# Attention in rounds of two units with shared banks and the division on POOL; alignment path coded by flags on DVE, PE and ACT

## The reference

```python
# layer 1: attention; latents = normalised x, keys and values from context and latents together
q = ln @ Wq                                   # 16 heads of 64
k, v = split(concat([xn, ln]) @ Wkv)          # 256 keys for each of the 64 sequences
w = softmax(q @ k.T / 8)
x = x + (w @ v) @ Wo
# layer 3: dynamic time warping of each context sequence against each x sequence
D = pairwise_euclidean(context, layernorm(x)) # 128 x 128
R[i, j] = D[i, j] + min(R[i-1, j], R[i, j-1], R[i-1, j-1])
# walk back from the last cell: diagonal before up before left on ties,
# and add context row i to output row j for every cell (i, j) on the way
```

## Time and profile before

| | |
|---|---|
| runs (3) | 3696.86, 3699.18, 3698.50 us; median 3698.5 us |
| profiled execution | 3698.72 us, span 3697.0 us |
| PE busy | 3236.4 us, 88% of the span |
| DVE busy | 2700.5 us, 73% |
| ACT busy | 1969.6 us, 53% |
| POOL busy | 1141.7 us, 31% |
| attention | to about 1970 us of the span |
| experts and distances | to about 2964 us |
| alignment | to about 3212 us |

### The profile page before, as it was taken

One profiled execution on the slowest core, in us unless ns is written; L12 is line 12 of the kernel. 1 busy time (PEld: TensorE's weight loads), 2 busy tenths in 40 slices (PEclk: granted clock), 3 DMA queues, 4 the chain that ended last, 5 costly groups with the idle time before them and its releaser, 6 DMA issues. The chain is left out here.

```text
span 3697.0 us, 64710 instructions
## 1 busy us (share of the span) xinstructions
PE 3236.4 (88%) x23172; PEld 2706.9 (73%) x23172; DVE 2700.5 (73%) x5786; ACT 1969.6 (53%) x5061; POOL 1141.7 (31%) x1116
## 2 busy tenths in 40 slices
PE   6999999999999999999996999999999800167786
PEld 5888888888888888888885888888888800055564
DVE  6777777777777777777765655665664979879997
ACT  4565656666565656565653333333333601099996
POOL 2222222222222222222211333333333200058888
PEclk9999999999999999999997999999999955588888
DMA  4000000000000000000002011101101740001101
GB/s 145 4 7 4 7 4 7 7 4 7 4 7 4 7 4 7 4 7 4 7 1 75 30 42 47 47 25 47 47 28 43 223 85 0 6 29 41 35 29 35
DMA packets 104171, 108.01 MB, mean 29 GB/s; under 512 B 7856, under 2 KB 85168, under 8 KB 103856
## 3 DMA queue, kind: packets, MB, share of 16 engines
q1 hardware_dynamic: 103856, 103.88, 9.5%
HBM read 90.75 MB, written 13.11 MB: 28 GB/s over the span
## 5 line engine op out<-in xcount | busy, mean ns | idle before, releaser
L619 POOL TENSOR_TENSOR attention_prob<-attention_prob,attention_inv_sums 128x512 f32<-128x512 f32 x256 | 266.7, 1042 | 1250.8 <-DVE attention_inv_sums L536 1250.8
L423 ACT ACTIVATE attention_prob<-attention_scores,attention_neg_max 128x256 f32<-128x256 f32 x1024 | 471.8, 473 | 142.9 <-DVE attention_neg_max L529 77.5
L406 ACT ACTIVATE attention_k_hi<-attention_proj 128x512 fp32r<-128x512 f32 x256 | 152.9, 597 | 554.5 <-PE attention_proj L277 554.5
L1068 POOL TENSOR_TENSOR experts_hidden_lo<-experts_weighed,experts_hidden_hi 128x512 fp32r<-128x512 f32 x192 | 252.2, 1313 | 551.1 <-ACT experts_hidden_hi L891 551.1
L539 DVE TENSOR_SCALAR attention_prob<-attention_prob,attention_inv_sums 128x256 f32<-128x256 f32 x512 | 398.1, 817 | 9.0
L546 DVE COPY attention_probT<-attention_turned 128x512 f32<-128x512 f32 x256 | 177.1, 692 | 294.9 <-PE attention_heads_out L331 294.9
L891 ACT ACTIVATE experts_hidden_hi<-experts_weighed 128x512 fp32r<-128x512 f32 x192 | 121.4, 632 | 424.1 <-DVE experts_weighed L1020 424.1
L529 DVE TENSOR_REDUCE attention_neg_max<-attention_scores 128x2 f32<-128x512 f32 x512 | 325.1, 675 | 3.4 <-PE attention_scores L303 3.4
L331 PE MATMUL attention_heads_out<-attention_probT,attention_v 128*64 128x128 f32 x4096 | 281.9, 280 | 1.6 <-DVE attention_attT_lo L553 1.6
L1015 DVE TENSOR_TENSOR experts_silu<-experts_silu,experts_spread 128x512 f32<-128x512 f32 x128 | 89.3, 698 | 259.4 <-ACT experts_silu L885 258.3
L315 PE MATMUL attention_turned<-ident,attention_prob 128*128 128x128 f32 x2048 | 265.4, 272 | 4.4 <-DVE attention_prob L539 4.4
(11 more groups left out here) (259 smaller groups left out, 9842.0 us busy)
## 6 DMA issues: line engine op xcount, KB each, us to landing
experts_spread<-shares SPq DMA_DIRECT2D x256, 128.0 KB, 3.0
x_all<-in_x SPq DMA_DIRECT2D x8, 1024.0 KB, 10.7
attention_ctx<-in_ctx SPq DMA_DIRECT2D x32, 256.0 KB, 2.7
distance_ctx<-in_ctx SPq DMA_DIRECT2D x16, 512.0 KB, 4.3
distance_ctxT<-in_ctxT SPq DMA_DIRECT2D x32, 256.0 KB, 4.8
weights_ctx<-in_ctx SPq DMA_DIRECT2D x16, 512.0 KB, 3.9
out<-conv_x_out SPq DMA_DIRECT2D x15, 512.0 KB, 3.0
dist<-distance_dist SPq DMA_DIRECT2D x16, 256.0 KB, 2.5
```

The costliest lines, as they stand in the source:

```text
L423: made = act.activation(prob[:, h, :], scores[e][:, m * 256:(m + 1) * 256], ACT.Exp, bias=neg_max[:, n % 2, 2 * e + m:2 * e + m + 1], accu ...
L619: pool.tensor_tensor(prob[:, 2:4, :], prob[:, 2:4, :], inv[:, n % 2, 2:4].unsqueeze(2).broadcast_to([P, 2, 2 * TOK]), ALU.mult).then_inc(d ...
L1068: pool.tensor_tensor(hid_lo[n % 3][:, :], weighed[n % 2], hid_hi[n % 3][:, :].bitcast(F32), ALU.subtract).then_inc(hid_split, 1)
```

## The change

Attention now goes in 128 rounds of two units. In round `u`, with `n = 2u`, PE does score(n), score(n+1), weigh_values(u-1) for both units of the last round in one group of 32 matmuls, project_k(n+2), project_q(u+1), project_k(n+3), then project_v and turn_probs twice, and in the first round of a pair both outputs of the last pair; turn_inputs stands at the end of the first two rounds of a pair.

The three `proj`, two `scores` and two `turned` banks become one rotation of seven banks `turns`; a user waits for the one seven places earlier. `prob` and `probT` have two buffers each. All four heads are divided on POOL, in one instruction of 1024 columns; DVE only inverts the sums. All four copies of a round from `turned` to `probT` are DVE's; ACT has none. The high and low parts of the weighed heads are made once a round with 512 columns. k has two buffers instead of three, v three homes instead of two buffers. All of norm_a, norm_b and norm_c of the next pair fall in the first round of a pair. x is waited for in four sets.

In the alignment a chunk is coded with flags in bf16: DVE makes `falls` (1152 columns) and `left` (1024) after the chunk; PE exchanges the halves of the partitions with four matmuls into `diag_ps`; six rows into the next chunk DVE makes `moved` (1024) and a multiply-and-add scan `back` (1024); PE takes the differences of neighbours in `back` with four matmuls, and ACT copies them to `rise`. The last chunk is finished after the last row. The ternary work on ACT stands between chunks.

```diff
-            for n in range(LAST + 4):
...
+            for u in range(ROUNDS + 1):
+                n = 2 * u
+                more = u + 1 < ROUNDS
+                if u < ROUNDS:
+                    score(n)
+                    score(n + 1)
+                if u:
+                    weigh_values(u - 1)
+                if more:
+                    project_k(n + 2)
+                    project_q(u + 1)
+                    project_k(n + 3)
+                for j in range(2):
+                    if more:
+                        project_v(n + 2 + j)
+                    if u < ROUNDS:
+                        turn_probs(n + j)
+                for b in outputs_in(u):
+                    output(b)
+                if late_input(u) is not None:
+                    turn_inputs(late_input(u))
...
-            def divide(n):
+            def invert(n):
                 dve.wait_ge(exped, n + 1)
+                if n >= 2:
+                    dve.wait_ge(divided, n - 1)
                 dve.reciprocal(inv[:, n % 2, :], sums[:, n % 2, :]).then_inc(inverted, 1)
-                dve.wait_ge(inverted, n + 1)
-                for h in range(2):
-                    made = dve.tensor_scalar(prob[:, h, :], prob[:, h, :], inv[:, n % 2, h:h + 1], None, ALU.mult)
-                made.then_inc(divided, 1)
...
+                if u < ROUNDS:
                     row_max(n)
+                    row_max(n + 1)
...
+                    if norm_next:
+                        norm_a(p + 1)
+                    invert(n)
+                    invert(n + 1)
+                if more:
                     low_k(n + 2)
+                if u:
+                    low_heads(u - 1)
+                if norm_next:
+                    norm_b(p + 1)
+                if more:
+                    low_q(u + 1)
+                    low_k(n + 3)
+                if u < ROUNDS:
+                    copy_probs(n)
+                    if norm_next:
+                        norm_c(p + 1)
+                    copy_probs(n + 1)
+                for b in outputs_in(u):
+                    add_out(b)
...
+            for u in range(ROUNDS):
+                p, i = divmod(u, QUADS)
+                if p + 1 < PAIRS and not i:
                     inverse_std(p + 1, 0, 4)
+                for n in (2 * u, 2 * u + 1):
+                    pool.wait_ge(inverted, n + 1)
+                    pool.tensor_tensor(prob[n % 2][:, :, :], prob[n % 2][:, :, :],
+                                       inv[:, n % 2, :].unsqueeze(2).broadcast_to([P, QH, 2 * TOK]), ALU.mult
+                                       ).then_inc(divided, 1)
+                if p + 1 < PAIRS and not i:
                     inverse_std(p + 1, 1, 2)
+                if late_input(u) is not None:
+                    low_inputs(late_input(u))
...
                 if (i + 1) % (2 * CH) == 0:
                     dve.wait_ge(row_made, i + 1)
-                    for part in coding:
-                        part(k // CH)
-                if i == N // 2:
+                    compare(k // CH)
+                if i % (2 * CH) == 5 and i > 2 * CH:
+                    trace(k // CH - 1)
+                if i == 84:
                     weights.means(dve)
+            trace(CHUNKS - 1)
```

More of the change, by code:

```diff
@@ L76, in attention @@
     PER_PAIR = 2 * QUADS
+    ROUNDS = LAST // 2
     XC = 8
+    X_SETS = (range(0, 1), range(1, 2), range(2, 4), range(4, 8))
     STAGES, PER_STAGE = 4, INNER // DIM
@@ L295, in score @@
                 pe.wait_ge(k_split, 2 * u + 2)
-                if n:
-                    pe.wait_ge(exped, n)
+                banks = [take_bank("s", 2 * n + e) for e in range(2)]
                 for h in range(QH):
```

430 lines of the change are left out of this document (226 added, 204 removed).

## The result

The changed kernel takes 3593.5 us (median of 4 runs, 3592.0 to 3595.0) against 3698.1 us (4 runs, 3696.9 to 3699.2): ratio 0.972, 95% interval 0.970 to 0.973. The forecast was 3641 with a range of 3570 to 3695: the right sign, inside the range, 47.5 us too long.

What follows compares the result with a forecast made beforehand. PE's own pace was taken to bound attention, DVE's dependent chain the alignment. From 3698.7 us: attention -94, PE standing in first rounds +62, alignment -26, sum -58, hence 3641 us; range 3570 to 3695.

Steps and rivals of the forecast that it cites:

- So about 0.1 goes wherever PE goes into or out of a group of another shape: PE in attention: each entry to or exit from a matmul group of another shape loses about 0.1 us.
- 12.03 + 0.60 = 12.63: Plain attention round on PE: bare work plus shape-change losses in us, 0.76 less than before, bounds 0.6 and 0.85.
- Values 2.05: Bare PE time in us taken for the values products of one two-unit attention round.
- PE stands 2.0 us: Pair's first round, last turning: PE waits for DVE's low q behind normalisations blocked by POOL's divisions; +62 us in total.
- not blocked: Rival: DVE's normalisation passes beside POOL's division, so PE never stands; 3579 us, chance 0.27.
- The two divisions of DVE ... cost nothing and give nothing: Attention round: taking DVE's two divisions off it changes no time, since PE is the bound.
- The values want the last copy at 1.6 and have it at 1.3: Attention round: DVE's last turned copy lands 0.3 us before PE's values need it, the round's smallest slack.
- Start and end of the stage at 0, outputs at +3: Attention: stage ends change nothing (bounds -4 and +4); outputs now following the turning cost 0.1 us a pair, +3.
- Alignment -26: Alignment: DVE's cheaper chunk coding saves 28.7 us, the uncovered last chunk adds 2.2; bounds -17 and -36.
- the 0.3 for the exchange: Alignment's last chunk: the part of PE's exchange, in us, that DVE's `left` does not hide.
- Waits, not shapes: Rival: PE's losses come from semaphore waits before groups, so grouping saves only 13 us; 3722 us, slower, chance 0.11.
- stopped elsewhere: Rival: attention is held up elsewhere, likeliest by late copies before the values; 3679 us, or 3710 with longer division, chance 0.12.

Runs made afterwards that it cites:

- kernels 5: Changed kernel with the next unit's k projection put back between the two units' scores; 3669.9 us, ratio 0.993 to the kernel before.
- 10: Changed kernel with low q and low k ahead of the normalisation, plus values split in two groups with a k projection between them; 3599.0 us, ratio 0.973.
- Kernels 4: Changed kernel with one more, already met, semaphore wait in the middle of each k and v projection; 3592.4 us, ratio 0.972.
- kernel 8: Changed kernel with low q and low k ahead of the normalisation, plus both v projections ahead of both turnings; 3554.3 us, ratio 0.962.
- Kernel 3: Changed kernel with DVE making low q and low k before the normalisation instead of after it; 3550.7 us, ratio 0.961.
- kernel 7: Changed kernel with the division shared again, DVE dividing heads 0 and 1 of each unit, POOL heads 2 and 3; 3563.2 us, ratio 0.964.
- kernel 9: Changed kernel with both low q and low k ahead of the normalisation and the division shared by DVE and POOL; 3547.7 us, ratio 0.959.
- kernel 2: The change's attention with the alignment of the kernel before; 3620.8 us, ratio 0.980.

## Why the prediction was right in sign and 47 us too long

Its mechanisms held, two of its sizes did not.

- **"So about 0.1 goes wherever PE goes into or out of a group of another shape": held in kind, and it is 0.19 for a change.** It was given as 0.1 an entry and 0.1 an exit, with turnings counted as a shape of their own. Six such losses, 0.60, were left in the changed round; three changes at 0.19 are 0.58, so this term came out right in sum. Counted by tile size alone, a round of before has 8 changes (each unit: into the scores, out of them, into the values, out of them) and one of the changed kernel 3 (turning to scores, scores to values, values to k). 5 fewer at (13.39 - 12.42) / 5 = 0.194 each; kernels 5 and 10 give 0.19 by adding two. In the starts it shows as the prediction's 0.1 in and 0.1 out: a score's first interval is 0.22 where the next are 0.12, the one from the last score product to the values is 0.22, and the first of the k behind the values is 0.35 in place of 0.23. Kernels 4 and 10 exclude the waits, kernel 8 the kind of product.
- **"12.03 + 0.60 = 12.63": the failed term.** The bare work is too high. "Values 2.05" is twice the distance from 16 values to the next group, which has a loss at its exit each time; the 0.1 at values to k was then added on top. One group of 32 takes 1.89, and with the k behind it 3.40 in place of 3.54. q was put at 12 x 0.118 = 1.42; its products start 0.113 apart and it takes 1.36. The scores with their losses take 1.64 in place of 1.72, the second k 1.37 in place of 1.39, and the two v and turnings 4.65 in place of 4.56. Together that is the error of 0.21; over 128 rounds 27 us. The 0.97 saved lies outside the bounds that were given for it, 0.6 and 0.85.
- **"PE stands 2.0 us": right in place, releaser and cause, too long by 0.6**, 18 us over 31. POOL's division is 1.90 as taken. But the divisions ran from 6.7 to 10.5 us of the round (which begins at 1019.43), not from 7.05 to 11.15: the sums came earlier, and DVE's instruction between the two divisions did not shove the second by 0.3 (POOL's second lasts 1.94, its first 1.90). Low q landed at 12.9 where the laid out round had 13.8. Kernel 3 shows cause and price (43 us). So the rival *not blocked*, which gave 3579, was wrong in its cause, though at 14.5 us from the measured time it was closer than the forecast. That was luck: it left out a stand of 44 us and saved 27 too little in the plain rounds, and the two errors cancel in part. With nothing standing the time is that of kernel 3, 3551.
- **POOL's division and what stands beside it.** The trace shows DVE's normalisation at 0.86 and 1.98 us beside POOL's divisions, each to 0.15 behind a division's end, and at 0.40 behind them; the rule of the Trainium skill that the second to come waits out the other's instruction ("SBUF — State Buffer", Who interferes with whom) agrees. The trace has 1.90 us for a division of 1024 columns; the 2.6 cycles an element of the Trainium skill ("GPSIMD Engine Reference", 3.1) made it an estimated 2.2, which is too much here. That page's advice, to leave two-input work on DVE, kernel 7 bears out by 30 us for half of the division, through DVE's wait; with low q early (kernel 9) it is worth nothing that shows.
- **"The two divisions of DVE ... cost nothing and give nothing"**: right (kernels 7 and 9). The consequence was not drawn: with that order of DVE, moving them to POOL was all price.
- **"The values want the last copy at 1.6 and have it at 1.3"**: right, with more room. In the round of 1064.68 DVE's last copy ends at 1065.71, 1.0 into it. The page of the changed kernel has 1.0 us of idle for the values in all 128 rounds (L345, released by the copies).
- **Start and end of the stage at 0, outputs at +3:** the sum of the new terms, 128 x 0.97 = 124 less 31 x 1.41 = 44, is 80, and the attention became 80.4 shorter. Nothing is left for either. The stages behind it took 2.1 us more here and about 1.5 less in kernel 2 with the same attention, so no effect of the change on them is shown.
- **Alignment -26: -28.0.** Around the first seven chunks, from row scan to row scan, the coding is 6.11 where it was 9.82. That is 3.71 less, 29.7 for eight (28.7 predicted). The last chunk gave back 1.75 where 2.2 was taken: the wait behind the scan is near the 1.85 predicted, but the 0.3 for the exchange did not come, since its matmuls ran two at a time (below) and were done at 3038.42, with DVE's `left` at 3038.44.
- *Waits, not shapes* (3722) and *stopped elsewhere* (3679 to 3710) did not happen. The one rotation of seven banks and the second buffers of `prob` and `probT` were not run by themselves; the five changes fewer leave no part of the plain round's 0.97 for them.

## What to carry to other kernels

When PE is the bound, count the places where the tile size of its products changes and group by it. In this kernel the count times one measured change gives the round, while kinds of product on the same tile size and waits that are already met cost nothing that showed. A group's measured length holds its entry or exit loss: take that out before adding losses of your own. Before giving work to POOL, look at which of DVE's instructions it keeps out and at what is queued behind them; putting the wanted low parts ahead of the blocked instruction was worth 43 us, more than the division's place.

## What was not expected of the hardware

- A change between tile sizes costs 0.19 us in the mean of the two that were added at each of two places, with the scores' 64*128 (12.42 to 12.79) as with the values' 128*64 (12.42 to 12.80), at a granted clock of 1.00. One kind of product after another on the same tile size has no such price (kernel 8).
- Cutting POOL's instruction in two does not let DVE through sooner: DVE's four normalisations took 3.42 us against 3.41.
- Not all of DVE's work is kept out by POOL's division: low q took 0.68 us beside it (kernel 3) where a normalisation took up to 1.98.
- Matmuls on two different 64*64 parts of the array ran side by side: the exchange's four products of 512 columns, 0.63 each, were done in 1.05 us (3037.36 to 3038.42) at a granted clock of 0.50, not in the 2.5 that were the bound. One behind the other at the 0.42 between the two pairs' starts, four would take an estimated 1.9 (3 x 0.42 + 0.63).

```profile
3037.36 0.63 PE L1422 MATMUL align_diagonal_ps<-align_falls,align_ident 64*64 64x512 bf16 x1 [7.27 <-DVE align_falls L1480]
3037.36 0.63 PE L1425 MATMUL align_diagonal_ps<-align_falls,align_ident 64*64 64x512 bf16 x1
...
3037.79 0.63 PE L1425 MATMUL align_diagonal_ps<-align_falls,align_ident 64*64 64x512 bf16 x1
```
